# Split-half products in place of fp32 matmuls in the down projections of experts 6 and 7

## The reference

```
h = item_feat @ W_item.T + b_item
b = layernorm(x) @ W_user.T + b_user
x = x + relu(adj @ h + b)
xf = layernorm(x)
probs = softmax(xf @ gate_w + gate_b);  cw = the two largest of probs, else 0
for e in 0..7:
    acc += cw[:, e] * (gelu(xf @ W1[e] + b1[e]) @ W2[e] + b2[e])
x = x + acc
```

## Time and profile before

| | |
|---|---|
| median of the three runs | 1711.62 us |
| the profiled execution: its own time, its span | 1713.0 us, 1711.2 us |
| PE busy | 1677.4 us, 98% of the span |
| DVE busy | 1466.2 us, 86% |
| ACT busy | 1239.5 us, 72% |
| moved by DMA | 423.73 MB, mean 248 GB/s |
| granted clock of PE, mean | 0.996 |

### The profile page before, as it was taken

One profiled execution on the slowest core, in us unless ns is written; L12 is line 12 of the kernel. 1 busy time (PEld: TensorE's weight loads), 2 busy tenths in 40 slices (PEclk: granted clock), 3 DMA queues, 4 the chain that ended last, 5 costly groups with the idle time before them and its releaser, 6 DMA issues.

```text
span 1711.2 us, 27009 instructions
## 1 busy us (share of the span) xinstructions
PE 1677.4 (98%) x7485; PEld 1356.6 (79%) x7485; DVE 1466.2 (86%) x2285; ACT 1239.5 (72%) x1601; POOL 69.6 (4%) x63
## 2 busy tenths in 40 slices
PE   7999999999999999999999999999999999999997
PEld 6767878788888888888888888878788888888874
DVE  4888989898989898888888888989898989898875
ACT  5767777677777777777777777777677777777764
POOL 1000000000000000000000000000000000000000
PEclk9999999999999999999999999999999999999999
DMA  7988877777777777878777787878777777777710
GB/s 237 362 301 288 259 252 256 249 263 254 248 262 252 257 255 250 265 244 267 244 258 240 259 257 252 253 253 256 252 261 255 249 259 255 257 252 252 265 43 13
DMA packets 124638, 423.73 MB, mean 248 GB/s; under 512 B 14261, under 2 KB 19894, under 8 KB 124618
## 3 DMA queue, kind: packets, MB, share of 16 engines
q1 hardware_dynamic: 120456, 415.41, 73.7%
q10 hardware_dynamic: 3314, 5.71, 0.9%
q0 software_dynamic: 848, 2.36, 0.4%
HBM read 418.31 MB, written 5.12 MB: 247 GB/s over the span
## 4 chain that ended last, share of the span: by engine, by line
PE 91%; DVE 4%; DMA 3%; ACT 2%; issue 1%; ACTq 0%; DVEq 0%; SPq 0%
PE acc L753 20%; PE acc L755 20%; PE acc L754 19%; PE ps_z L826 4%; PE ps_z L827 4%; PE ps_z L828 4%; PE ps_y L785 4%; PE ps_y L779 3%; PE ps_y L781 3%; PE ps_y L780 3%; DMA raw<-in_adj_main 2%; PE ps_w L836 2%; DVE a_lo L527 2%; PE acc L771 1%; PE ps_x L761 1%; PE ps_g L803 1%
## 5 line engine op out<-in xcount | busy, mean ns | idle before, releaser
L527 DVE TENSOR_TENSOR a_lo<-raw,a_hi 128x1000 fp32r<-128x1000 f32 (+1 forms) x800 | 930.1, 1182 | 134.3 <-ACT a_hi L375 129.5
L375 ACT ACTIVATE a_hi<-raw 128x1000 fp32r<-128x1000 f32 (+1 forms) x800 | 801.1, 1026 | 226.4 <-PE acc L755 187.1
L753 PE MATMUL acc<-a_hi,h_hi 128*128 128x500 f32 x1580 | 648.0, 410 | 10.7 <-DVE a_lo L527 7.0
L755 PE MATMUL acc<-a_hi,h_lo 128*128 128x500 f32 x1580 | 617.5, 391 | 0.0
L754 PE MATMUL acc<-a_lo,h_hi 128*128 128x500 f32 x1580 | 615.2, 389 | 0.0
L753 PEld LDWEIGHTS acc<-a_hi,h_hi 128*128 128x128 f32 x1580 | 298.9, 189 | 87.2 <-issue 19.2
L754 PEld LDWEIGHTS acc<-a_lo,h_hi 128*128 128x128 f32 x1580 | 298.8, 189 | 66.3 <-issue 12.8
L755 PEld LDWEIGHTS acc<-a_hi,h_lo 128*128 128x128 f32 x1580 | 297.8, 188 | 60.7
L440 ACT ACTIVATE g_sb<-ps_z,b_sb 128x500 f32<-128x500 f32 x320 | 198.6, 672 | 83.8 <-DVE gs_lo L664 78.4
L664 DVE TENSOR_TENSOR gs_lo<-g_sb,gs_hi 128x500 fp32r<-128x500 f32 x240 | 151.7, 673 | 38.9 <-PE ps_y L781 37.7
L655 DVE TENSOR_TENSOR g_sb<-ps_w,g_sb 128x500 f32<-128x500 f32 x240 | 151.0, 670 | 7.8 <-ACT g_sb L440 7.8
(11 more groups left out here) (121 smaller groups left out, 1067.9 us busy)
## 6 DMA issues: line engine op xcount, KB each, us to landing
raw<-in_adj_main SPq DMA_DIRECT2D x780, 500.0 KB, 4.5
xr_sb<-in_xR SPq DMA_DIRECT2D x20, 250.0 KB
x_sb<-in_xT SPq DMA_DIRECT2D x20, 250.0 KB, 2.7
out<-r_sb ACTq DMA_DIRECT2D x20, 250.0 KB, 4.2
raw<-in_itemT SPq DMA_DIRECT2D x13, 384.0 KB, 3.4
g_sb<-in_w POOLq DMA_DIRECT2D x4, 250.0 KB, 5.7
raw<-in_adj_rem SPq DMA_DIRECT2D x20, 31.2 KB, 2.9
r_sb<-in_w POOLq DMA_DIRECT2D x2, 250.0 KB, 5.7
```

The source lines that it names most:

```text
L375: nc.scalar.activation(a_hi[q][0:rows, 0:cols], raw[s][0:rows, 0:cols], ACT.Copy).then_inc(hi_ready, 1)
L527: nc.vector.tensor_tensor(a_lo[q][0:rows, 0:cols], raw[s][0:rows, 0:cols], val(a_hi[q][0:rows, 0:cols]), ALU.subtract).then_inc(lo_ready, 1)
L753: nc.tensor.matmul(acc[:, 0:T], w_hi, m_hi, start=(k == 0), stop=False)
L755: last = nc.tensor.matmul(acc[:, 0:T], w_lo, m_hi, start=False, stop=(k == KT))
```

## The change

Experts 6 and 7 do what experts 0 to 5 do. Their `W2` is held as halves `w2_hi`, `w2_lo`; the direct load of their fp32 part in the constants is gone, and the pieces of the split grow from nine to ten (the ninth from 36 to 500 columns, and a tenth of 48). DVE's L655 writes `g_sb` for all experts; ACT at s+6 and DVE at s+7 form `gs_hi` and `gs_lo` of experts 6 and 7 too, and PE's down projection of these two moves from s+6 to s+8, that is from p = 20 and 25 to p = 22 and 27. The wait of L655 of expert 7 for the down projection of expert 6 is gone, and the gelu of expert 7 waits for the `gs_lo` of expert 6. The buffers `gs_sb` and `w2_sb` are gone.

```diff
-NSPLIT = 6
-
-DOWN = [8 if e < NSPLIT else 6 for e in range(E)]
+DOWN = 8
...
-        w2_hi = sb("w2_hi", [P, NSPLIT * HH * D], fp32r)
-        w2_lo = sb("w2_lo", [P, NSPLIT * HH * D], fp32r)
-        w2_sb = sb("w2_sb", [P, (E - NSPLIT) * HH * D])
+        w2_hi = sb("w2_hi", [P, E * HH * D], fp32r)
+        w2_lo = sb("w2_lo", [P, E * HH * D], fp32r)
...
-        w2_pieces = pieces(NSPLIT * HH * D)
+        w2_pieces = pieces(E * HH * D)
...
-                  (gate_b_sb, gate_b_rows), (b1_sb, b1), (w2_sb, w2[:, NSPLIT * HH * D:]),
+                  (gate_b_sb, gate_b_rows), (b1_sb, b1),
                   (before_sb, before)]
...
                     if not (isinstance(i, int) and i == 1 and e == 0):
 
-                        if 0 < e <= NSPLIT:
-                            act.wait_ge(gs_lo_ready, i * (NSPLIT * HH) + HH * (e - NSPLIT))
-                        else:
-                            act.wait_ge(gs_ready, i * (E * HH) + HH * (e - E))
+                        act.wait_ge(gs_lo_ready, i * (E * HH) + HH * (e - E))
                     for j in range(HH):
...
-                if p - A_SCALED in STARTS[:NSPLIT]:
+                if p - A_SCALED in STARTS:
                     e = STARTS.index(p - A_SCALED)
...
                     dve.wait_ge(spread_done, i * E + (e + 1 - E))
-                    if e > NSPLIT:
+                    for j in range(HH):
+                        dve.wait_ge(gelu_ready, i * (E * HH) + (HH * (e - E) + j + 1))
+                        nc.vector.tensor_tensor(g_sb[j][:, :], ps_w[:, 0:T], g_sb[j][:, :],
+                                                ALU.mult).then_inc(gs_ready, 1)
+                if p - V_SCALED in STARTS:
+                    e = STARTS.index(p - V_SCALED)
+                    if not (isinstance(i, int) and i == 1 and e == 0):
 
                         dve.wait_ge(down_done, i * E + (e - E))
                     for j in range(HH):
-                        dve.wait_ge(gelu_ready, i * (E * HH) + (HH * (e - E) + j + 1))
-                        scaled = g_sb[j] if e < NSPLIT else gs_sb[j]
-                        nc.vector.tensor_tensor(scaled[:, :], ps_w[:, 0:T], g_sb[j][:, :],
-                                                ALU.mult).then_inc(gs_ready, 1)
-                if p - V_SCALED in STARTS[:NSPLIT]:
...
             def down(i, e):
                 for j in range(HH):
-                    if e < NSPLIT:
-
-                        pe.wait_ge(gs_lo_ready, i * (NSPLIT * HH) + (HH * (e - NSPLIT) + j + 1))
...
-                    else:
-                        pe.wait_ge(gs_ready, i * (E * HH) + (HH * (e - E) + j + 1))
-                        n = (e - NSPLIT) * HH + j
-                        last = nc.tensor.matmul(ps_y[:, 0:T], w2_sb[:, n * D:(n + 1) * D], gs_sb[j][:, :], start=False,
-                                         stop=(e == E - 1 and j == HH - 1))
+
+                    pe.wait_ge(gs_lo_ready, i * (E * HH) + (HH * (e - E) + j + 1))
+                    cols = slice((e * HH + j) * D, (e * HH + j + 1) * D)
+                    nc.tensor.matmul(ps_y[:, 0:T], w2_hi[:, cols], gs_hi[e % 2][j][:, :], start=False, stop=False)
+                    nc.tensor.matmul(ps_y[:, 0:T], w2_hi[:, cols], gs_lo[j][:, :], start=False, stop=False)
+                    last = nc.tensor.matmul(ps_y[:, 0:T], w2_lo[:, cols], gs_hi[e % 2][j][:, :], start=False,
+                                            stop=(e == E - 1 and j == HH - 1))
                 last.then_inc(down_done, 1)
...
-                    if p != STARTS[e] + DOWN[e]:
+                    if p != STARTS[e] + DOWN:
                         continue
```

More of the change, by code:

```diff
@@ L147, in build @@
         gs_hi = [[sb(f"gs_hi{s}_{j}", [P, T], fp32r) for j in range(HH)] for s in range(2)]
-        gs_sb = [sb(f"gs_sb{j}", [P, T]) for j in range(HH)]
         gs_lo = [sb(f"gs_lo{j}", [P, T], fp32r) for j in range(HH)]
@@ L175, in build @@
         w_ready = sem("w_ready")
-        w2_landed = [sem(f"w2_landed{n}") for n in range(-(-NSPLIT * HH * D // T))]
+        w2_landed = [sem(f"w2_landed{n}") for n in range(-(-E * HH * D // T))]
         power_ready = sem("power_ready")
@@ L648, in experts @@
                     dve.wait_ge(spread_done, i * E + (e + 1 - E))
-                    if e > NSPLIT:
-                        dve.wait_ge(down_done, i * E + (e - E))
                     for j in range(HH):
                         dve.wait_ge(gelu_ready, i * (E * HH) + (HH * (e - E) + j + 1))
-                        scaled = g_sb[j] if e < NSPLIT else gs_sb[j]
-                        nc.vector.tensor_tensor(scaled[:, :], ps_w[:, 0:T], g_sb[j][:, :],
+                        nc.vector.tensor_tensor(g_sb[j][:, :], ps_w[:, 0:T], g_sb[j][:, :],
                                                 ALU.mult).then_inc(gs_ready, 1)
-                if p - V_SCALED in STARTS[:NSPLIT]:
+                if p - V_SCALED in STARTS:
                     e = STARTS.index(p - V_SCALED)
@@ L662, in experts @@
                     for j in range(HH):
-                        dve.wait_ge(gs_hi_ready, i * (NSPLIT * HH) + (HH * (e - NSPLIT) + j + 1))
+                        dve.wait_ge(gs_hi_ready, i * (E * HH) + (HH * (e - E) + j + 1))
                         nc.vector.tensor_tensor(gs_lo[j][:, :], g_sb[j][:, :], val(gs_hi[e % 2][j][:, :]),
```

## The result

The changed kernel takes 1716.63 us, the median of 8 runs (1712.18 to 1720.21), against 1711.98 for the kernel before (8 runs, 1707.44 to 1714.06): ratio 1.0023, 95% interval 1.0012 to 1.0034. It is a little slower. The profiled execution took 1720.2 us, the slowest of the eight, with a span of 1718.4.

What follows compares the result with a forecast made beforehand. PE was taken to bound the 18 alike passes, a chain of waits the drain. From the profiled execution, 1713.0 - 3.2 + 4.3 + 0.8 = 1714.9; from the median, 1711.6 + 1.9 = 1713.5, range 1704.5 to 1717.5.

Steps and rivals of the forecast that it cites:

- The PE gain: In the 18 passes, split products of two experts take 2.70 us instead of 3.35, so PE gains 0.65 per pass.
- The first pair is free: In the passes, expert 6's two gs_lo (1.18 us on DVE) cost nothing, covered by 1.18 of idle time that goes.
- The wait at position 27: In the passes, expert 7's gs_lo pair makes PE wait for DVE's subtraction, 0.47 us per pass (0.3 to 0.6).
- Rival A: DVE's lead suffices, PE never waits at position 27: 11.7 us less over the passes, 1705.0 in all; chance 0.17.
- rival C: L655 of expert 7 is late, PE waits 1.65 us at position 27: 18 us more, 1734.7; chance 0.08.
- Nothing is late behind it: In the passes after position 27, later positions, drain of ps_y and loads cost nothing; expert 0's gelu moves by 0.1 us.
- The drain, by its chain: After the passes, longer waits cost 3.7 us in block 19 and 0.6 in block 20, 4.3 more (3 to 6).
- Pass 0: In the first pass, larger weight pieces and 0.25 MB of moved weights cost 0.8 us, between 0 and 1.4.
- rival B: In the drain, PE's clock falls after a longer idle stretch, slowing thirteen matmuls: some 2.5 us, 1716.0; chance 0.14.

Runs made afterwards that it cites:

- late_lo7: The changed kernel with the gs_lo pair of expert 7 formed on DVE one position later, behind position 27's subtraction: 1706.68 us, ratio 0.9964 to the kernel before.
- wait_back: The changed kernel with the old wait put back, L655 of expert 7 waiting for expert 6's down projection: 1763.0 us in one run.
- late_fp32_drain_warm: The changed kernel with expert 7's gs_lo behind position 27, fp32 matmuls for experts 6 and 7 in the drain, extra unread matmuls there: 1698.69 us, ratio 0.9928.
- after_again: The changed kernel measured once more, unedited: 1714.51 us, ratio 1.0014 to the kernel before.
- warm_drain: The changed kernel with extra matmuls, their results unread, filling five idle stretches of PE in the drain: 1711.38 us, ratio 0.9997 to the kernel before.

## Why the prediction came out as it did

**The PE gain** of 0.65 us per pass was right: 0.66, from the middle pass of late_lo7, in which PE does not wait. It was read from the starts of four L785 records and the matmul behind them, not from their mean of 584 ns, which overlaps.

**The first pair is free** by the idle time of the wait that goes. By the rows this is right: L644 starts without idle time, and no position from 22 to 26 waits. wait_back (+2.48 us) shows that the wait, had it stayed, would have cost time.

**The wait at position 27**: right in place, cause and size. 0.47 per pass was taken; late_lo7 gives 81.50 - 81.03 = 0.47. Pass forecast near 81.5, measured 81.49. Rival A (81.04, no wait) and rival C (82.7) fall by this row.

**Nothing is late behind it**: right for PE. Two loads became the last thing ACT waits for, without effect.

**The drain, by its chain**: 4.3 forecast, 4.2 between the two kernels without half clock. Its first part, `r_sb` of block 19, was put 3.7 later and came 3.6 later (28.8 against 25.2 us behind the addition of the residual, which the prediction calls its subtraction, in those two kernels). The rest, 0.6 for block 20, was 0.6.

**Pass 0**: 0.8 was taken; nothing is to be seen of it. The start of pass 2 is 177.7 us in the mean of the ten profiled executions with the new pieces and 177.6 in the two without. Three of the ten are 2 to 3 us late and neither of the two is, which is too few to rule a cost out. It stays open.

**The half clock**: this is the term that was mis-sized. It stood as rival B, a case of 0.14 that costs 2.5 us when it strikes. The place was well seen: in all six profiled executions of the changed chain without extra matmuls PE idles 2.1 to 3.5 us ahead of the last down projection of block 19, and the clock is low right there, for 5 to 12 matmuls where B had thirteen. (In the first profile it had fallen before, at 1665.7.) So it is not a case but a cost in every profiled execution: 3.3 us in the mean of five drains (wait_back's, with its other wait, left out). But the kernel before pays it too. With the old chain the drains without extra matmuls are 63.3, 65.0, 64.9 and 63.1 us, in the mean 2.3 over the 61.8 of late_fp32_drain_warm. The starting point of the sum had this cost in it, so what the change adds is the difference, some 1.0 us. From few executions, this is rough. The mean clocks point the same way: 9 of the 12 runs of after_again have one under what 27 of 29 runs of the kernel before have.

**The sum.** Measured, it reads -3.4 for the passes (18 x 0.19), +4.2 for the chain, some +1.0 for the clock and nothing seen for pass 0: +1.8. The forecast was +1.9, after_again measured +1.9, and this agreement is in part luck: 0.8 for pass 0, of which nothing is seen, stands where the clock's 1.0 should. The first measurement gave +4.7, 3.1 above the forecasted 1713.5 at 1716.6; that is inside the range and just beyond the 0.2% on the slower side, which had 0.27. Six of its eight runs have mean clocks of 0.990 to 0.994 and took 1716.5 us or more, the two at 0.995 and 0.996 took 1712 to 1713. Why long stretches at half clock were more frequent in it, no run shows.

## What to carry to other kernels

On a saturated PE, price added work on a feeding engine by its lead at each position, from two timelines laid side by side: the first 0.6 us cost nothing and the next 0.6 cost 0.5, at one place. An added step belongs behind the item that PE waits for next, not ahead of it; moving it by one position was worth 8 us here. And at a program's end, where no engine is full, price an added step by the chain of waits: the new steps cost 3.6 us in block 19, where they held up `r_sb` and all behind it, and only 0.6 in block 20, where an old wait went with them.

## What was not expected of the hardware

In the drain TensorE's clock went to half in each of the ten profiled executions without extra matmuls, for 6 to 29 matmuls, and in differing places in executions of one program. Ahead of each fall PE had idled, by rows of 1.95 to 3.5 us, but such a row is no sure sign: after_again's row of 2.64 us is followed by none, while behind the same row of the first profile the clock is low from the first matmul on (below, the first profile, then after_again; 0.49 is the record at full clock behind a wait).

```profile
1689.09 0.63 PE L810 MATMUL ps_z<-xn_hi,w_hi 128*128 128x500 f32 x1 [2.64 <-ACT g_sb L433]
```

```profile
1683.65 0.49 PE L810 MATMUL ps_z<-xn_hi,w_hi 128*128 128x500 f32 x1 [2.64 <-ACT g_sb L433]
```

A few matmuls without use, laid into the idle time, left no record at half clock in the two profiled drains that had them, and the median fell by 3.1 us in warm_drain. The Trainium skill ("TensorE: Matmul & The Clock Gate", section "HAM oscillation — how this bites in real kernels") has the rule that idle gaps between bursts bring the half clock. These traces agree in part, with 0.50 between 1665.7 and 1678.8 behind an idle row of 1.97; but a burst does not always start at half speed, as the prediction put the rule. In that profile the burst begins at full speed at 1664.09 and falls some 1.3 us later, and in the kernel before, the burst of 1683.40 does so after 0.8 us.
